# A graph network's result: from transposing back on TensorE to forming it in place on VectorE

## What is computed

```python
h = jnp.maximum(_layernorm(x, axis=-1), 0.0)
A = (adj != 0).astype(x.dtype)
for l in range(5):
    m = jnp.einsum('bnd,de->bne', h, weight[l])
    agg = jnp.einsum('bij,bid->bjd', A, m)
    h = _gru_cell(agg, h, w_ih, w_hh, b_ih, b_hh)   # r, z, n; h = (1 - z) * n + z * h
return x + h * mask[..., None]
```

## Time and profile before

| | us |
|---|---|
| median of 3 runs | 392.88 (392.7 to 392.98) |
| profiled execution, its own time | 393.39 |
| its span | 391.5 |
| TensorE busy | 374.1 |
| VectorE busy | 319.3 |
| ScalarE busy | 296.4 |
| GpSimd busy | 236.0 |

### The profile page before, as it was taken

How to read it: one execution, slowest core, us unless ns; L and a number is a source line. 1 busy time by engine, 2 the same in 40 slices (tenths; PEclk the granted TensorE clock), 3 DMA queues, 4 the chain that set the end, 5 groups by cost and what they waited for, 6 DMA issues and landing times.

```text
span 391.5 us, 6689 instructions
## 1 busy us (share of the span) xinstructions
PE 374.1 (96%) x2246; PEld 196.1 (50%) x2246; DVE 319.3 (82%) x630; ACT 296.4 (76%) x489; POOL 236.0 (60%) x215
## 2 busy tenths in 40 slices
PE   6868999999999999999999999999999999999991
PEld 2434555555555555555555555555555555555551
DVE  5775988988878799888888889878887877877885
ACT  3687889988978876989888877787777777777650
POOL 4445797797755656696958764464456554664221
PEclk9999999999999999999999999999999999999996
DMA  8726346357521634355444550315343333322222
GB/s 239 180 43 135 58 105 136 84 104 136 123 67 26 110 80 109 81 125 103 89 91 83 105 85 27 56 27 109 62 100 80 81 56 73 63 55 54 47 62 82
DMA packets 109361, 34.55 MB, mean 88 GB/s; under 512 B 84336, under 2 KB 109168, under 8 KB 109328
## 3 DMA queue, kind: packets, MB, share of 16 engines
q1 hardware_dynamic: 108912, 33.63, 41.5%
q10 hardware_dynamic: 288, 0.39, 0.4%
q0 software_dynamic: 128, 0.10, 0.1%
HBM read 9.21 MB, written 4.19 MB: 34 GB/s over the span
## 4 chain that ended last, share of the span: by engine, by line
PE 89%; DVE 4%; DMA 3%; ACT 1%; issue 1%; POOL 1%; DVEq 0%; POOLq 0%
PE ps_r L233 9%; PE ps_z L234 8%; PE ps_r L234 8%; PE ps_r L235 8%; PE ps_z L235 8%; PE ps_z L233 8%; PE ps_s L276 4%; PE ps_s L275 4%; PE ps_in L235 4%; PE ps_hn L234 4%; PE ps_in L234 4%; PE ps_in L233 4%; PE ps_hn L235 4%; PE ps_hn L233 4%; DMA hp<-nat 2%; PE ps_t L284 2%
## 5 line engine op out<-in xcount | busy, mean ns | idle before, releaser
L649 POOL TENSOR_TENSOR zh<-z,h 128x512 f32<-128x512 f32 x80 | 101.7, 1271 | 127.9 <-ACT z L392 127.5
L386 ACT ACTIVATE r<-ps_r,b_sum,unscale 128x512 f32<-128x512 f32 x80 | 62.3, 779 | 55.7 <-PE ps_r L235 53.8
L500 DVE SCALAR_TENSOR_TENSOR rhn<-ps_hn,b_hn,r 128x512 f32<-128x512 f32 x80 | 60.0, 750 | 21.1 <-ACT r L386 21.0
L506 DVE TENSOR_TENSOR ps_in<-ps_in,rhn 128x512 f32<-128x512 f32 x80 | 56.0, 700 | 23.6 <-PE ps_in L235 21.2
L396 ACT ACTIVATE ps_in<-ps_in,b_ih,unscale 128x512 f32<-128x512 f32 x80 | 60.1, 751 | 19.0 <-DVE ps_in L506 17.7
L654 POOL TENSOR_TENSOR hp<-h,hp 128x512 f16<-128x512 f32 x64 | 74.1, 1157 | 0.4 <-ACT hp L402 0.4
L512 DVE SCALAR_TENSOR_TENSOR ps_in<-z,ps_in 128x512 f32<-128x512 f32 x80 | 55.2, 691 | 8.3 <-ACT ps_in L396 8.2
L516 DVE TENSOR_TENSOR h<-zh,ps_in 128x512 f32<-128x512 f32 x80 | 55.0, 688 | 8.3
L392 ACT ACTIVATE z<-ps_z,b_sum,unscale 128x512 f32<-128x512 f32 x80 | 61.6, 770 | 0.0
L496 DVE TENSOR_TENSOR s_lo<-ps_s,s_hi 128x512 f16<-128x512 f32 x80 | 54.5, 681 | 0.0
L380 ACT CAST s_hi<-ps_s 128x512 f16<-128x512 f32 x80 | 46.7, 584 | 3.0 <-PE ps_s L276 1.0
(11 more groups left out here) (85 smaller groups left out, 735.2 us busy)
## 6 DMA issues: line engine op xcount, KB each, us to landing
x_all<-in_x SPq DMA_DIRECT2D x16, 256.0 KB, 4.5
adj_in<-in_adj SPq DMA_DIRECT2D x16, 256.0 KB, 4.2
out<-x_all SPq DMA_DIRECT2D x16, 256.0 KB, 2.4
nat<-hp SPq DMA_TRANSPOSE x64, 3.1
fold_in<-in_fold_lhs SPq DMA_DIRECT2D x1, 320.0 KB, 4.8
hp<-nat SPq DMA_TRANSPOSE x15, 3.2
whh_sb<-in_w_hhT ACTq DMA_DIRECT2D x1, 192.0 KB, 3.2
wih_sb<-in_w_ihT ACTq DMA_DIRECT2D x1, 192.0 KB, 4.2
```

What stands on the lines that cost most here:

```text
L386: nc.scalar.activation(r[:], ps_r[:], ACT.Sigmoid, bias=b_sum[:, 0:1], scale=unscale[:, 0:1]).then_inc(r_done, 1)
L500: nc.vector.scalar_tensor_tensor(out=rhn[:], in0=ps_hn[:], scalar=b_hn[:, 0:1], in1=r[:], op0=ALU.add, op1=ALU.mult).then_inc(rhn_done, 1)
L506: nc.vector.tensor_tensor(ps_in[K % 2][:], ps_in[K % 2][:], rhn[:], ALU.add).then_inc(npre_done, 1)
L649: nc.gpsimd.tensor_tensor(zh[:, K % 2], z[:, K % 2], h[:, t % RING], ALU.mult).then_inc(zh_done, 1)
```

## The change

The result is formed where the state already lies, with features on partitions. The host hands over x a second time, transposed (`xT`, features by all nodes), and the mask as one row (`mask_row`), and turns the output back. The TensorE transposes of the final step (`transpose_last`) and its four pieces on VectorE are gone.

In a unit of the last layer, L516's counterpart writes zh - ps_in into ps_in itself, and `result(K)` follows it at once on VectorE with two whole 128x512 instructions: mask times ps_in into ps_in, then x plus ps_in into `x_out`. TensorE's next products into that bank wait for `out_done` instead of `h_done`. `x_out` and `mask_in` are rings of six tiles, filled by two loads for each tile (`load_ends`), six units ahead; the mask's load repeats its row on all partitions. The x of the normalisation lies in a ring of eight (`x_in`).

The very last unit has its own form. TensorE makes the z product ahead of r, and hn behind both; ScalarE takes z before r and puts tanh into r's buffer; GpSimd multiplies the tile's h by the mask five units before the end, and adds z times that to x; VectorE forms (z - 1) * mask before the tanh is there, then multiplies by n and subtracts from x; ScalarE's queue stores the tile.

The diff, cut to its core:

```diff
-    ends = {}
-    for t in range(TILES):
-        soon = min(at[t, LAST] + 2, N - 1) if t < TILES - 1 else N
-        ends[t] = soon if t >= starts[-1] else max(soon, ends[t - 1] + 3 if t else 0)
+    ends = {t: at[t, LAST] for t in range(TILES - 1)}
     tile_at_stage = [{prep[t] + s: t for t in prep} for s in range(STAGES)]
-    ending = {K: [t for t in ends if ends[t] == K] for K in range(N + 1)}
+    ending = {ends[t]: t for t in ends}
+    fetching = {ends[t] - FETCH: [t] for t in ends}
+    fetching[N - FINISH - FETCH].append(TILES - 1)
 
     x_t = x.rearrange("(t g) n d -> t n g d", g=TG)
     adj_t = adj.rearrange("(t g) i j -> t i g j", g=TG)
-    out_t = out.rearrange("(t g) n d -> t n g d", g=TG)
+    xT_t = xT.rearrange("d (t c) -> t d c", c=TILE)
+    mask_t = mask_row.rearrange("(t c) -> t c", c=TILE)
+    out_t = out.rearrange("d (t c) -> t d c", c=TILE)
 
...
+            def load_ends(t):
+                f = t % FRING
+                if t >= FRING:
+                    sp.wait_ge(stored[f], 16 * (t // FRING))
+                sp.dma_start(x_out[:, f], xT_t[t]).then_inc(ends_loaded[f], 16)
+                sp.dma_start(mask_in[:, f], mask_t[t].partition_broadcast(P)).then_inc(ends_loaded[f], 16)
+
             def store(t):
                 sp.wait_ge(out_done, t + 1)
-                sp.dma_start(out_t[t], x_all[:, t].rearrange("p (g d) -> p g d", g=TG)).then_inc(stored, 16)
+                sp.dma_start(out_t[t], x_out[:, t % FRING]).then_inc(stored[t % FRING], 16)
 
...
                     pe.wait_ge(hp_loaded[t % RING], 16 * (t // RING + (t % RING >= DIRECT)))
                 else:
                     pe.wait_ge(h_lo_done, inner[at[t, l - 1]])
+                if K == N - 1:
+                    pe.wait_ge(z_done, K)
+                    h_product(K, 1, ps_z)
                 if K:
                     pe.wait_ge(r_done, K)
                 h_product(K, 0, ps_r)
-                if K:
-                    pe.wait_ge(z_done, K)
-                h_product(K, 1, ps_z)
+                if K < N - 1:
+                    if K:
+                        pe.wait_ge(z_done, K)
+                    h_product(K, 1, ps_z)
+                else:
+                    last_products(K)
+                    return
                 if K:
                     pe.wait_ge(rhn_done, K)
                 h_product(K, 2, ps_hn)
@@ -260,6 +281,15 @@
                 t, l = units[K]
                 return three(ps, block_of(v_hi[:, l], k), block_of(v_lo[:, l], k),
                              s_hi[:, K % 2], s_lo[:, K % 2], k == 2, True)
+
+            def last_products(K):
+                pe.wait_ge(s_lo_done, K + 1)
+                s_product(K, 1, ps_z).then_inc(z_mm, 1)
+                s_product(K, 0, ps_r).then_inc(r_mm, 1)
+                pe.wait_ge(rhn_done, K)
+                h_product(K, 2, ps_hn).then_inc(last_hn_mm, 1)
+                pe.wait_ge(out_done, units[K - 2][0] + 1)
+                s_product(K, 2, ps_in[K % 2]).then_inc(in_mm, 1)
 
             def aggregate(K):
...
-            def transpose_last(t):
-                pe.wait_ge(h_done, at[t, LAST] + 1)
-                if t > starts[-1]:
-                    pe.wait_ge(out_done, t - 1)
-                elif t:
-                    pe.wait_ge(out_done, t)
-                for q in range(TG):
-                    last = nc.tensor.transpose(block_of(ps_end(t), q), block_of(h[:, t % RING], q), ident_sb[:])
-                last.then_inc(f_mm, 1)
-
...
+                elif K >= 2:
+                    pe.wait_ge(out_done, units[K - 2][0] + 1)
                 s_product(K, 2, ps_in[K % 2]).then_inc(in_mm, 1)
                 if folding(K):
                     fold(folding(K))
-            for K in (N - 1, N):
-                for t in ending[K]:
-                    transpose_last(t)
 
...
-                    act.wait_ge(f_mm, t - RING + 1)
+                    act.wait_ge(masked, t - RING + 1)
...
-                nc.scalar.activation(ps_in[K % 2][:], ps_in[K % 2][:], ACT.Tanh, bias=b_ih[:, 2:3],
+                n = ps_in[K % 2] if K < N - 1 else r
+                nc.scalar.activation(n[:], ps_in[K % 2][:], ACT.Tanh, bias=b_ih[:, 2:3],
...
+            def store_last():
+                t = TILES - 1
+                act.wait_ge(last_out, 1)
+                act.dma_start(out_t[t], x_out[:, t % FRING]).then_inc(stored[t % FRING], 16)
...
-                nc.vector.tensor_tensor(h[:, t % RING], zh[:, K % 2], ps_in[K % 2][:], ALU.subtract).then_inc(h_done, 1)
-
-            def final(t):
-                if t == 0:
-                    dve.wait_ge(mask_loaded, 16)
-                dve.wait_ge(f_mm, t + 1)
-                for q in range(TG):
-                    x_q = block_of(x_all[:, t], q)
-                    last = nc.vector.scalar_tensor_tensor(
-                        out=x_q, in0=block_of(ps_end(t), q), scalar=mask_sb[:, t * TG + q:t * TG + q + 1],
-                        in1=x_q, op0=ALU.mult, op1=ALU.add)
-                last.then_inc(out_done, 1)
+                out_ap = h[:, t % RING] if units[K][1] < LAST else ps_in[K % 2][:]
+                nc.vector.tensor_tensor(out_ap, zh[:, K % 2], ps_in[K % 2][:], ALU.subtract).then_inc(h_done, 1)
+
+            def result(K):
+
+                t = units[K][0]
+                f = t % FRING
+                dve.wait_ge(ends_loaded[f], 32 * (t // FRING + 1))
+                dve.wait_ge(h_done, K + 1)
+                nc.vector.tensor_tensor(ps_in[K % 2][:], mask_in[:, f], ps_in[K % 2][:], ALU.mult).then_inc(masked, 1)
+                dve.wait_ge(masked, t + 1)
+                nc.vector.tensor_tensor(x_out[:, f], x_out[:, f], ps_in[K % 2][:], ALU.add).then_inc(out_done, 1)
+
+            def masked_open(K):
+
+                f = units[K][0] % FRING
+                dve.wait_ge(z_done, K + 1)
+                dve.wait_ge(last_h_masked, 1)
+                nc.vector.scalar_tensor_tensor(out=ps_s[:], in0=z[:, K % 2], scalar=1.0, in1=mask_in[:, f],
+                                               op0=ALU.subtract, op1=ALU.mult).then_inc(open_done, 1)
+
+            def last_result(K):
+
+                f = units[K][0] % FRING
+                dve.wait_ge(n_done, K + 1)
+                dve.wait_ge(open_done, 1)
+                nc.vector.tensor_tensor(ps_in[K % 2][:], ps_s[:], r[:], ALU.mult).then_inc(zn_done, 1)
+                dve.wait_ge(zn_done, K + 1)
+                dve.wait_ge(last_kept, 1)
+                nc.vector.tensor_tensor(x_out[:, f], x_out[:, f], ps_in[K % 2][:], ALU.subtract).then_inc(last_out, 1)
 
...
-                for t in ending[K]:
-                    final(t)
-                new_state(K)
+                if K < N - 1:
+                    new_state(K)
+                else:
+                    masked_open(K)
+                    last_result(K)
+                if units[K][1] == LAST and K < N - 1:
+                    result(K)
                 if folding(K):
                     v_low(folding(K))
-            for K in (N,):
-                for t in ending[K]:
-                    final(t)
 
         @block.gpsimd
         def _(pool):
@@ -644,6 +693,8 @@
                 pool.wait_ge(z_done, K + 1)
...
                 t = units[K][0]
                 pool.wait_ge(h_hi_done, inner[K])
                 nc.gpsimd.tensor_tensor(h_lo(t), h[:, t % RING], h_hi(t), ALU.subtract).then_inc(h_lo_done, 1)
+
+            def masked_last_h():
+                t = TILES - 1
+                pool.wait_ge(ends_loaded[t % FRING], 32 * (t // FRING + 1))
+                pool.wait_ge(h_lo_done, inner[at[t, LAST - 1]])
+                nc.gpsimd.tensor_tensor(h[:, t % RING], mask_in[:, t % FRING], h[:, t % RING],
+                                        ALU.mult).then_inc(last_h_masked, 1)
+
+            def kept_result(K):
+                f = units[K][0] % FRING
+                pool.wait_ge(zh_done, K + 1)
+                nc.gpsimd.tensor_tensor(x_out[:, f], x_out[:, f], zh[:, K % 2], ALU.add).then_inc(last_kept, 1)
 
             def first():
                 nc.gpsimd.memset(eps[:], EPS).then_inc(consts_set, 1)
...
             for K in range(N):
                 kept(K)
+                if K == N - 1:
+                    kept_result(K)
                 if K < FIRST - 2:
                     natural_low(K + 2)
                 if K and units[K - 1][1] < LAST:
@@ -683,6 +747,8 @@
                     adjacency(tile_at_stage[2][K])
                 if K in tile_at_stage[5]:
                     natural_low(tile_at_stage[5][K])
+                if K == N - FINISH:
+                    masked_last_h()
 
```

More of the change, by code:

```diff
@@ L22 @@
 LN = 3
-XSEM = 8
+XRING = 8
+FRING = 6
 DIRECT = 1
+FETCH = 6
+FINISH = 5
 STAGES = 9
@@ L122, in gnn_kernel @@
         ps_s, ps_t, ps_f = bank("ps_s"), bank("ps_t"), bank("ps_f")
-        x_loaded = [sem(f"x_loaded{i}") for i in range(XSEM)]
+        x_loaded = [sem(f"x_loaded{i}") for i in range(XRING)]
```

(23 more changed lines are left out.)

55 lines of the change are left out of this document (32 added, 23 removed).

## The result

The changed kernel took 398.39 us (median of 4 runs, 398.23 to 399.98), the kernel before 392.93 beside it (4 runs, 392.7 to 394.9). The ratio is 1.0135, 95% interval 1.0108 to 1.0162: slower by some 1.4%, where 398.9 had been forecast. Its profiled execution took 398.33, with a span of 396.0, against 391.5 before. All executions on these pages were in the usual, fast state but one of the split kernel (e8), which took 1172.8 us and is left out.

What follows compares the result with a forecast made beforehand. TensorE, busy 96%, was taken as the bound. Group 0 (units 16 to 19) +2.0, group 1 (44 to 49) +3.7, group 2 (74 to 79) with tail +0.3: +6.0 on 393.39 gives 399.4, less 0.5 398.9; range 397.0 to 400.9.

Steps and rivals of the forecast that it cites:

- The mechanism: Units 16 to 19, 44 to 49, 74 to 78: VectorE idle only for tanh, TensorE waiting for s_lo, 5.37 us each.
- The pair: Two new VectorE instructions per last-layer unit, behind the new state: 0.69 to 0.70 us each, 1.60 together, nothing hiding them.
- no step of 4.77 elsewhere: Sign of being right: outside the last-layer stretches units take 4.33 us, none 4.77.
- The rule weighed: On VectorE, a semaphore wait between dependent instructions costs nothing extra; rejected on 0.61 against 0.80 us; its rival, 387.3, chance 3%.
- The tail: Last unit, from last n input (385.72) to end (391.76): shorter tail saves 3.5 us; group 2 with it nets +0.3.
- the store: Last tile's store from ScalarE's queue, up to the span's end: 3.03 us, bounds 0.3 less or 0.3 more.
- The shift of unit 48: Shift on VectorE in group 1: taken at nothing, could cost up to 0.6 us.
- the DMA: Added x and mask loads, tight at unit 13's transpose: taken at nothing, 1.1 us kept for the range.
- The median: Median of the runs taken as 0.5 us below the profiled execution: 399.4 becomes 398.9.
- TensorE as the bound: Rival: in last-layer units the pair costs VectorE no more than its 0.57 us of waiting; about 383.7, chance 4%.
- Late transposes: Rival: unit 13's transpose lands too late (+1.1) and unit 48's shift waits (+0.6); 400.6, chance 12%.
- The clock: Rival: TensorE's clock falls to 1.2 from 2.4 GHz in the three last-layer stretches; about 448, chance 2%.

Runs made afterwards that it cites:

- e8: Changed kernel with the pair split: GpSimd multiplies h by the mask, VectorE adds x in tanh's shadow, late waits first, group 0's loads moved; 388.31 us, 0.9870 of the kernel before.

## Why the prediction was right

**The mechanism** held: VectorE idle only for the tanh, TensorE waiting for `s_lo`, units of 4.33 us behind groups 0 and 1 where final steps had stood (units 21 to 29 and 51 to 73), 2.97 us from the last n input (390.37) to the end of VectorE's work (393.34). The pair on 8 columns showed that its time is the whole loss; the pair in the shadow, that its place makes it dearer: of the 0.52 us a unit gained there, 0.31 are cover and 0.21 a dependent step that is gone. The shadow had no more to give, as `s_lo` stood in it already. One sign was stated too widely: "no step of 4.77 elsewhere". Such steps stand in units 5, 8, 11, 30, 34, 38 and 42 of both kernels, where TensorE turns a later tile's normalised x (L314 in the changed kernel); they are no part of the sum. The 0.69 to 0.70 us for each new instruction, taken from the earlier trace rows, is what the groups by line have: a mean of 696 ns for the 15 of L555, 686 for the 15 of L557.

**The rule weighed** falls, for a follower that waits on a semaphore: the Trainium skill, "VectorE: DVE Perf Modes", section "The DRAIN you can't avoid", has such a wait cost nothing beyond the pipe's emptying. The rows have 0.60 to 0.61 us for a follower that needs nothing, 0.73 for a dependent one with its late wait first, and 0.80 with another wait ahead of it.

**The sizes that were off**, all to the same side. The pair: its second step is 0.73 and not 0.80, so a unit 5.30 and not 5.37. Over 15 units that is 1.05 us of the 1.5 by which the span was forecast too long (+6.0, measured +4.5). I had put the 0.80 down to the dependence alone; 0.07 of it is the order of its waits. The tail: 5.63 us from the last n input to the end against 6.04, 0.07 of it the same step again, and the rest the store, 2.66 from the end of VectorE's work against the 3.03 taken; I had named 0.3 less as a bound and did not use it, and no run had shown either bound. The shift of unit 48 cost nothing and the DMA cost nothing, as taken.

**The median** came out 0.5 us below the forecast although the span was 1.5 below. The time around the span was 2.33 us (398.33 - 396.0) against the 1.9 carried over, and the median lay 0.06 above the profiled time against the 0.5 below that I had subtracted. So 1.0 us of the agreement is luck.

**The rivals.** TensorE as the bound (383.7) needed the pair under 1.20 us; it is 0.80 + 0.73 = 1.53. Once the pair was tiny or elsewhere, the time was near that rival's: 384.7 and 385.5. Late transposes exist, but not in either trace of the changed kernel. The clock stayed at 1.00 of 2.4 GHz in the three groups: at 380 to 385 us TensorE was busy 4.43 of 5 us and the granted clock was 1.00.

## What to carry to other kernels

A busy share cannot price an addition: 82% before and after, and the kernel went from bound by TensorE to bound by VectorE in 15 of 80 units. Price it in the unit where it lands, as a chain with each step's own pitch, and ask which waiting time can cover it there; here the same two instructions cost 13.4 us of span uncovered, 5.7 in the tanh's shadow (388.3 - 382.6), and next to nothing on another engine once they were laid where its queue had room (spans of 382.4 to 382.6 in four of six executions; the waits stand in the better order there too, and what that gave was not separated).
